# A fourth row-by-row fetch beside 116 gathers in an embedding and dot-interaction kernel

## What is computed

```python
e = jnp.stack([tbl_0[ids[:, 0]], ..., tbl_31[ids[:, 31]]], axis=1)   # 512 x 32 x 256
dots = jnp.einsum('bnd,bmd->bnm', e, e)
z = dots[:, iu, ju]                                # i < j: 496 products a sample
h = jnp.concatenate([z, dense_ctx], axis=1)
h = jnp.maximum(h @ W_top1 + b_top1, 0.0)          # 512
h = jnp.maximum(h @ W_top2 + b_top2, 0.0)          # 256
y = h @ W_top3                                     # 512 x 1
```

## Time and profile before

| | us |
|---|---|
| median of 3 executions | 166.62 |
| the profiled execution's time | 166.71 |
| its span, first to last instruction | 164.8 |
| outside the span | 1.9 |
| TensorE busy in the span | 141.4 (86%) |
| GpSimd busy in the span | 112.5 (68%) |

### The profile page before, as it was taken

How to read it: one execution, slowest core, us unless ns; L and a number is a source line. 1 busy time by engine, 2 the same in 40 slices (tenths; PEclk the granted TensorE clock), 3 DMA queues, 4 the chain that set the end, 5 groups by cost and what they waited for, 6 DMA issues and landing times.

```text
span 164.8 us, 7924 instructions
## 1 busy us (share of the span) xinstructions
PE 141.4 (86%) x3214; PEld 119.9 (73%) x3214; DVE 91.4 (55%) x277; ACT 46.5 (28%) x143; POOL 112.5 (68%) x124
## 2 busy tenths in 40 slices
PE   6996996989799895699999694899894799999884
PEld 6995974778598684688988472589662788978673
DVE  3191335369738485186757742377776164746652
ACT  0003010414021540224625411056361220616240
POOL 4777777777777777777777777777777777774000
PEclk9999999999999999999999999599999579999999
DMA  1499579875846734457676544343334333333000
GB/s 43 149 328 326 175 218 334 272 254 178 289 116 177 220 106 124 121 170 219 192 237 192 163 128 114 106 115 116 104 109 135 107 105 113 109 99 99 4 4 4
DMA packets 11300, 25.44 MB, mean 154 GB/s; under 512 B 2958, under 2 KB 4574, under 8 KB 11264
## 3 DMA queue, kind: packets, MB, share of 16 engines
q0 software_dynamic: 5616, 15.34, 30.9%
q10 hardware_dynamic: 4860, 9.14, 17.4%
q1 hardware_dynamic: 788, 0.46, 1.0%
HBM read 24.71 MB, written 0.00 MB: 150 GB/s over the span
## 4 chain that ended last, share of the span: by engine, by line
PE 43%; DMA 26%; POOL 12%; DVE 8%; issue 6%; ACTq 3%; ACT 1%
DMA rows<-tables,idx 24%; POOL rows L402 12%; PE xt_ps L420 10%; PE hot_ps L471 8%; PE gram_ps L435 8%; PE act_ps L501 5%; PE dve_ps L501 3%; PE hot_ps L520 2%; DVE z L328 2%; ACTq L807 2%; DVE z L321 2%; DVE xt L337 2%; DMA z<-z 1%; PE act_ps L578 1%; PE gram_ps L520 1%
## 5 line engine op out<-in xcount | busy, mean ns | idle before, releaser
L402 POOL DMA_INDIRECT rows<-tables,idx x117 | 111.7, 955 | 37.0 <-issue 25.6
L420 PE MATMUL xt_ps<-ident,rows 128*128 128x128 f32 x232 | 41.4, 288 | 11.7 <-DMA rows<-tables,idx 11.5
L420 PEld LDWEIGHTS xt_ps<-ident,rows 128*128 128x128 f32 x232 | 27.3, 145 | 17.9 <-DMA rows<-tables,idx 16.0
L337 DVE COPY xt<-xt_ps 128x512 f32<-128x512 f32 (+1 forms) x32 | 21.8, 682 | 33.4 <-PE xt_ps L420 33.0
L471 PE MATMUL hot_ps<-mask,hot_sb 128*128 128x128 f32 x256 | 35.9, 286 | 3.4 <-ACT hot_xt L844 3.4
L471 PEld LDWEIGHTS hot_ps<-mask,hot_sb 128*128 128x128 f32 x256 | 30.7, 191 | 4.6 <-issue 3.5
L435 PEld LDWEIGHTS gram_ps<-xt 128*32 128x32 f32 x1920 | 21.4, 113 | 12.6 <-issue 9.6
L435 PE MATMUL gram_ps<-xt 128*32 128x32 f32 x1920 | 28.3, 200 | 1.7 <-DVE xt L337 1.5
L348 DVE COPY last_xt<-xt_ps 128x64 f32<-128x64 f32 x28 | 7.7, 274 | 24.2 <-PE xt_ps L420 23.8
L321 ACT COPY z<-gram_ps 32x128 f32<-32x128 f32 (+1 forms) x56 | 19.4, 346 | 5.0 <-PE gram_ps L435 4.2
L321 DVE COPY z<-gram_ps 32x128 f32<-32x128 f32 (+1 forms) x56 | 19.2, 342 | 0.9
(11 more groups left out here) (70 smaller groups left out, 81.2 us busy)
## 6 DMA issues: line engine op xcount, KB each, us to landing
single_rows<-tables SPq DMA_DIRECT2D x320, 1.0 KB
hot_sb<-hot_tables ACTq DMA_DIRECT2D x8, 512.0 KB, 5.0
w_sb<-w ACTq DMA_DIRECT2D x8, 256.0 KB
rows<-tables,idx POOLq DMA_INDIRECT x117
w_packed_sb<-w_packed ACTq DMA_DIRECT2D x5, 256.0 KB
single_rows<-tables ACTq DMA_DIRECT2D x64, 1.0 KB
hot_ids_sb<-hot_ids ACTq DMA_DIRECT2D x2, 256.0 KB, 4.3
w_sb<-w ACTq DMA_DIRECT2D x1, 512.0 KB
```

Of the source, the lines that this page charges most:

```text
L337: return copy(xt[:, bank, :, places].rearrange("p k l q f -> p k (l q f)"), xt_ps[:, bank, :, places].rearrange("p k l r -> p k (l r)"))
L402: pool.indirect_dma_start(rows[:, n % RING, :], None, tables, bass.IndirectOffsetOnAxis(idx[:, fetch:fetch + 1], 0)).then_inc(rows_landed[ ...
L420: last = nc.tensor.transpose(xt_ps[:, fetch // 2 % 2, k, fetch % 2, :], x[:, P * k:P * (k + 1)], ident[:])
```

## The change

`SINGLE` gets a fourth fetch: fetches 43, 85, 117 and 113 go row by row, in this order, where it was 43, 83 and 109. SyncE issues 362 rows (all of 43 and 85, and 106 of 117) where it was 320. ScalarE issues 150 rows (22 of 117, then all of 113) where it was 64, and three a pair in pairs 4 to 53 where it was two a pair in pairs 10 to 41. Its blocks of 32 offsets begin at its rows 0, 32, 64, 96 and 128, which are due in pairs 4, 14, 25, 36 and 46; before, they began in pairs 10 and 26. 116 gathers are left, and fetches 83 and 109 are among them.

```diff
-SINGLE = (43, 83, 109)
-SP_ROWS = 320
+SINGLE = (43, 85, 117, 113)
+SP_ROWS = 362
 ACT_ROWS = P * len(SINGLE) - SP_ROWS
-ACT_ROW_PAIRS = range(10, 42)
+ACT_ROW_PAIRS = range(4, 54)
 LOAD = 32
```

## The result

The changed kernel took 194.88 us in the median of 4 executions (193.58 to 195.38), the kernel before 166.31 us (165.41 to 167.21): 1.169 times as long, 95% interval 1.163 to 1.174. The forecast was 169.3 us with a range up to 171.5. The direction was right, and the size was wrong by a factor of eleven: 28.6 us lost where 2.6 were forecast.

What follows compares the result with a forecast made beforehand. It took TensorE's backlog behind fetch 89 and block 2's moves, not gathers, to bound the kernel. Block 1's moves 2.3, less 0.8 at fetch 89, plus 1.1 for pair 45's rows gave 2.6 us on 166.71: 169.3 us, range 167.3 to 171.5.

Steps and rivals of the forecast that it cites:

- The bound: End of the kernel: set by fetch 89, block 2's moves and TensorE's backlog, not gathers; one gather less gains 0.
- Where the loads fall: ScalarE's five block starts fall in pairs 4, 14, 25, 36 and 46; pairs 25 and 36 are the ones to watch.
- What a block's start costs: ScalarE's queue: beginning a block of offsets costs 2.5 us, read from pair 10, and everything behind it waits.
- TensorE's waits for gathers eat it up: After unit 7, TensorE's 3.5 us delay shrinks by 0.7 us up to 94 us; fetch 89's wait takes another 0.8.
- the ring never held it up: GpSimd's gathers in the kernel before: idle 0.3 us at most, so it issues without a stop and runs on.
- Hidden: pairs 4, 14 and 46: Starts in pairs 4 and 14 hidden by ScalarE's waits of 9.14 and 6.66 us, pair 46's by over 4 us.
- Pair 45's rows: Three rows between block 2's second and third move make the landing 1.1 us later (0.9 to 1.4).
- SyncE: 362 rows put its last row's start at 151.3 us; fetch 117 costs nothing with TensorE 2.6 us late.
- A, the clock: Rival: a longer wait before block 1's network or in pair 26 halves TensorE's clock, 1.5 us more, 170.8 us; chance 0.22.
- B: Rival: delays absorbed, block 1's moves land in time, only pair 45's or SyncE's last rows count, 167.8 us; chance 0.20.
- C: Rival: the end hangs on fetches 118 and 119, so one gather less gains 1.25 us, 165.5 us; chance 0.07.
- D: Rival: the clock is not halved after the wait for block 2's moves, 165.2 or 165.0 us; chance 0.05.

Runs made afterwards that it cites:

- e12: Kernel before with only fetches 43 and 83 row by row, all 256 rows on SyncE, none on ScalarE, 118 gathers: 165.7 us against 166.4, ratio 0.997.
- e13: Kernel before with ScalarE's rows in pairs 9 to 40 instead of 10 to 41, so its second offset load stands in pair 25: 166.2 us, ratio 0.998.
- e14: Kernel before with ScalarE's rows in pairs 9 to 40 and its offsets beginning at element 330 instead of 320: 175.0 us, ratio 1.049.
- e1: Changed kernel with ScalarE's offsets beginning at element 384 instead of 362: 239.9 us against 233.0 for the kernel before, on a slow chip, ratio 1.047.
- e2: Kernel before with ScalarE's 64 offsets beginning at element 330 instead of 320: 233.0 us in both medians, on a slow chip, ratio 1.012.
- e3: Kernel before with SyncE's ten offset blocks 0 to 24 elements past multiples of 64: loads fast at 0, 4, 8, 12, 16, 24, slow at 1, 2, 3, 6.
- e8: The kernel before, unchanged, executed once for its trace on a chip of the slow kind: 230.4 us.

## Why the prediction was wrong

**The bound.** Right, as far as the runs show: the end hangs on TensorE's backlog, ScalarE and the moves, and the gather taken away gained nothing. Fetch 118 is transposed at 182.9 us, 11.8 us after its gather's start; e12 has one gather more at no cost.

**Where the loads fall.** Right for pairs 25, 36 and 46, and the waits of unit 7, of block 1's products and moves, and of block 2's moves are those that it named.

**What a block's start costs: the step that failed.** It said "a block's start costs 2.5 us" and measured it on a block that began at element 320. The changed blocks begin at 362 + 32k, and there the load alone took 7.1 us. The term entered twice with 2.5 and belongs in with some 7.4 (in pair 25 the gap between two rows is 7.2 us, in pair 36 it is 7.6 us from move to row). By the prediction's own sum the loss is then not 2.6 but 12.3 us (an estimate: 7.7 us late at block 1's first move, 12.0 at its network, less 0.8, plus 1.1). Three more starts that were put at nothing, in pairs 4, 14 and 46, stopped TensorE for 5.3, 4.7 and 1.0 us, because the cover had been measured against 2.5 us too. And where the sum let a term shrink again on its way to the end, there was nothing left for it to be paid from. The diff changes `SP_ROWS` from 320 to 362 and the table is cut there; that the cut moves the address of every load on ScalarE stood in the diff, and I hadn't asked what the address might do.

The page "Runtime: NRT & Kernel Launch" of the Trainium skill, section "Instruction fetch mechanics", gives register loads some 200 ns a register, even in bulk; it speaks of uncached loads, and the offsets here lie in SBUF. The trace of before, which has 32 in 2.1 us, doesn't follow it, so I had no reason to expect it. The slow loads here come near it: between the one of 22 (5.03 us) and one of 32 (7.12 us) lie 0.21 us for each further register. Between the loads from multiples of 4 elements, of 10 (1.21 us) and of 32 (2.12 us) lie 0.04 us each. The page's figure alone would make all of them slow; the runs show that the place decides.

**"TensorE's waits for gathers eat it up."** Right as a mechanism, and in e13 stronger than reckoned: 4.1 us late at unit 7, of which the prediction would have let 0.7 be paid back up to 94 us and 0.8 at fetch 89, and no loss. e13 also bears out two of its numbers for a load of 2.2 us: the wait in front of unit 7 is 2.55 us (about 3 us said), and block 1's first move starts at 98.09 us (98.0 said). But these waits are a sum that can be spent once: 11.5 us in all, 5.8 us of them behind unit 7. Four stalls of 4.7 to 8.0 us spent 8.2 us of it; the other 3.3 us lie ahead of the first stall. It was also said that "the ring never held it up", of a kernel whose stalls were at most 3.15 us; with longer ones the ring did stop GpSimd, at no cost that TensorE's waits show.

**Hidden: pairs 4, 14 and 46.** Wrong. The load of pair 4 was to be covered by ScalarE's wait of 9.14 us until 30.28 us, and it did end at 28.8 us. But the tables and rows of four pairs were queued behind it, another 5 us, which I had not added up against that wait; the copy came at 34.28 us, and TensorE waited 5.28 us for it. The load of pair 14 had less cover than the 6.66 us said: ScalarE was idle for that long, but its queue issued weights and rows in that time. In the changed kernel the queue came to the load at 47.37 us, and the lookup that the copy waits for ended at about 50.3 us, so that some 3 us of 7.13 were covered. Behind the load of pair 46 (155.8 to 160.9 us) stand six rows and copies, and ScalarE's next step that TensorE needs came 1.0 us late; this load is on the chain that ended last.

**Pair 45's rows.** Right in size: three rows stand between the second and third move, 152.32 to 153.35 us, 1.0 us where 1.1 was said. The first was the dear one, although SyncE had started its last row at 151.0 us; so here it isn't SyncE's issuing that makes it dear, as the prediction read rows 7. Three dear rows, 1.4 us, didn't come about, but SyncE issuing at the same time, which they were to come from, was not given either. The wait for the moves grew to 3.99 us ("over 3 us").

**SyncE.** Right: its last row started at 151.0 us (151.3 said). ScalarE's DMAs hardly slowed it. Fetch 117 waited for nothing.

**The rivals.** A, the clock: it did fall more often, and that explains little of the loss. The mean granted clock fell from 0.969 to 0.894 of full: (1 - 0.894) x 2 x 193.3 = 41 us at half clock (1.2 of 2.4 GHz), 10 us before. The slices show where: low digits from about 29, 53, 72, 87, 121 and 155 us on, each at one of the stalls. But much of this time TensorE stood idle, and all its work together took only 3.0 us longer. B, C and D didn't happen.

**What the 28.6 us are made of.** The timelines tell how late TensorE is at the same places of its program, in us:

| TensorE starts | before | changed | late |
|---|---|---|---|
| lookup unit 2 | 31.44 | 34.99 | 3.6 |
| unit 4 | 48.22 | 55.84 | 7.6 |
| unit 6 | 67.28 | 76.07 | 8.8 |
| unit 7 | 75.20 | 93.23 | 18.0 |
| network of block 1 | 106.95 | 131.68 | 24.7 |
| network of block 2 | 128.84 | 156.78 | 27.9 |
| end of the span | 164.8 | 193.3 | 28.5 |

It was to be 3.5, 2.3 and 2.6 us late at unit 7, at the network of block 1 and at the end. Each large step stands behind one of the slow loads. Summed by what TensorE waited for, the 28.5 us of the span are 18.4 us more in front of lookups, 8.2 in front of products of pairs (7.75 of them at block 1's), 3.7 for moves, 3.4 in small waits and 3.0 of longer work, less the 8.2 us that it no longer waited for gathers. e14, with two slow loads, returned 90% of their excess as time. The five loads' excess over loads from such places is 4.9, 4.9, 4.9, 5.3 us and, for the one of 22, 3.0 us (its time in e1 taken off): 23 us, and by that share some 20 us, an estimate. The other 8 us exceed the 2.6 us of the sum. The kernel with offsets in place never ran on a chip of this kind, and on the slow kind its loss was 4%. So whether 169 us would have been right with 2.2 us loads stays open.

## What to carry to other kernels

A duration read from the trace belongs to its operands' addresses too. When a constant moves where a table is cut, look up every instruction whose first address it shifts, and keep blocks that are loaded into registers at multiples of 16 bytes: the price was a factor of 3.3 for each load. Registers, loads and other work of a sequencer don't count as busy and don't stand in the timeline; a query by source line shows them, and a gap in the queue tells that one should be made.

A stall of TensorE can be paid back, but only out of its own waits that lie behind the stall. Sum them before a delay is written off as absorbed, take off what earlier delays have already spent, and price a term at both sides of the point where the sum is gone.

## What the runs showed of the hardware that I had not expected

A load of 32 offsets from SBUF into registers takes 2.0 to 2.6 us if its first 4-byte element lies on a multiple of 4 elements and 6.5 to 7.5 us if not, on SyncE and on ScalarE (the changed kernel, e1, e2, e3). The same kernel took 166 us on some chips and 228 to 233 us on others. There TensorE, in the middle of 32 short products, stood still for some tenths of a microsecond about once a pair with nothing in the profile that released it, 73 times and 36.1 us in all (e8). The cause was not looked for.
